# Perceiver block: first cross-attention in two groups of heads, the second group's maxima taken inside the first group's pass

## The reference

```python
q = (x @ Wq + bq).reshape(B, N, 16, 16)      # 128 queries, 16 heads of 16
k = (y @ Wk + bk).reshape(B, M, 16, 16)      # M = 12544 keys
v = (y @ Wv + bv).reshape(B, M, 16, 16)
scores = einsum('bnhd,bmhd->bhnm', q, k) * 0.25
out = einsum('bhnm,bmhd->bnhd', softmax(scores, -1), v).reshape(B, N, 256)
return relu(out @ W1 + b1) @ W2 + b2
```

## Time and profile before

| what | value |
|---|---|
| median of 3 runs | 1448.72 us (1447.15 to 1449.62) |
| span of the profiled execution | 1446.7 us, 2.0 us under that median |
| busy share of the span | PE 93%, ACT 77%, DVE 74%, POOL 14% |
| chain that ended last | PE 77%, DVE 13%, issue 5%, ACT 3% |
| first attention, first pass | to 258.2 us |
| first attention, second pass | 258.2 to 462.5 us |

### The profile page before, as it was taken

The page is one execution under the profiler, slowest core; times in us unless marked ns, Lnnn a source line. Parts: engine busy times, 40 slices in busy tenths (PEclk is TensorE's granted clock), DMA queues, the critical chain, the costliest instruction groups (busy, mean ns, idle before and its releaser), DMA issues.

```text
span 1446.7 us, 37819 instructions
## 1 busy us (share of the span) xinstructions
PE 1352.2 (93%) x15593; PEld 886.5 (61%) x15593; DVE 1072.6 (74%) x1556; ACT 1120.0 (77%) x1646; POOL 197.9 (14%) x195
## 2 busy tenths in 40 slices
PE   5888888999999998999999979999999999999988
PEld 2444444677776694333333357777777777777768
DVE  6899999100000777999999998888888888788864
ACT  4787877899997466888888868888887888788831
POOL 6322311000000006000000000000000004431630
PEclk9999999999999999999999999999999999999999
DMA  4355434876755564556655576777877588898910
GB/s 144 137 190 186 159 137 145 210 178 147 184 140 155 198 226 149 191 190 227 219 186 189 187 149 133 145 140 154 154 153 146 115 172 181 169 187 170 237 54 5
DMA packets 128849, 236.56 MB, mean 164 GB/s; under 512 B 9292, under 2 KB 114214, under 8 KB 128678
## 3 DMA queue, kind: packets, MB, share of 16 engines
q1 hardware_dynamic: 128678, 234.13, 61.1%
HBM read 155.98 MB, written 78.12 MB: 162 GB/s over the span
## 4 chain that ended last, share of the span: by engine, by line
PE 77%; DVE 13%; issue 5%; ACT 3%; DMA 1%; SPq 1%; POOL 0%; POOLq 0%; DVEq 0%; ACTq 0%
PE ps L794 77%; DVE small L1573 4%; DVE W L1507 3%; DMA W<-in_ctx_dram 1%; DVE p L1507 1%; ACT W L1311 1%; DVE W L1537 1%; DVE q_all L1507 1%; ACT p L1326 1%; DVE ctxT_b L1559 0%; DVE q_all L1817 0%; ACT p L1288 0%; ACT ps L1288 0%; DVE ctxT_a_lo L1563 0%; DVE v L1507 0%
## 5 line engine op out<-in xcount | busy, mean ns | idle before, releaser
L1507 DVE TENSOR_TENSOR p<-ps,p 128x512 f16<-128x512 f32 (+1 forms) x467 | 350.9, 752 | 66.2 <-ACT ps L1288 63.1
L1288 ACT ACTIVATE p<-ps 128x512 f16<-128x512 f32 (+1 forms) x490 | 329.4, 682 | 83.4 <-PE ps L794 81.0
L794 PEld LDWEIGHTS ps<-q_all,W 128*128 128x128 f16 (+1 forms) x3544 | 228.8, 99 | 71.5 <-issue 12.7
L794 PE MATMUL ps<-q_all,W 128*128 128x128 f16 (+2 forms) x3544 | 262.5, 226 | 8.8 <-DVE p L1507 5.3
L1288 ACT ACTIVATE ps<-ps 128x512 f32<-128x512 f32 x392 | 236.0, 602 | 0.0
L794 PE MATMUL ps<-v,p 128*128 128x130 f16 x3136 | 169.3, 206 | 6.3 <-DVE p L1507 2.7
L794 PE MATMUL ps<-wv,ctxT_a_hi 128*128 128x512 f16 (+1 forms) x588 | 155.3, 345 | 10.1 <-DVE W L1537 5.9
L794 PEld LDWEIGHTS ps<-v,p 128*128 128x128 f16 x3136 | 147.3, 97 | 12.7 <-ACT ps L1288 4.0
L1674 DVE COPY att<-ps 128x512 f32<-128x512 f32 x1 | 0.7, 692 | 201.6 <-PE ps L794 201.6
L1507 DVE TENSOR_TENSOR v<-ps,v 128x512 f16<-128x512 f32 x196 | 135.5, 692 | 12.9 <-ACT v L1384 0.5
L794 PE MATMUL ps<-wv,ctxT_b 128*128 128x512 f16 (+1 forms) x504 | 136.1, 338 | 0.1
(11 more groups left out here) (276 smaller groups left out, 2005.4 us busy)
## 6 DMA issues: line engine op xcount, KB each, us to landing
W<-keys_hi SPq DMA_DIRECT2D x54, 896.0 KB, 8.0
W<-keys_low SPq DMA_DIRECT2D x27, 896.0 KB, 11.5
keys_hi<-p SPq DMA_DIRECT2D x75, 224.0 KB, 1.9
keys_low<-p SPq DMA_DIRECT2D x75, 224.0 KB, 1.9
keys_hi<-W SPq DMA_DIRECT2D x65, 224.0 KB, 1.9
keys_low<-W SPq DMA_DIRECT2D x65, 224.0 KB, 1.9
W<-values SPq DMA_DIRECT2D x14, 960.0 KB, 9.2
W<-in_L_ffn_W_dram SPq DMA_DIRECT2D x10, 1024.0 KB, 10.0
```

The costliest lines, as they stand in the source:

```text
L794: return pe.matmul(out_, lhsT, rhs, start=start, stop=stop, **kw)
L1288: return act.activation(out_, in_, ACT.Exp, scale=scale)
L1507: return dve.tensor_tensor(out_, a, b, op)
```

## The change

The first attention's heads become two groups, 0-7 and 8-15.

- **First pass:** `ORDER0` has four pairs a round in place of eight; only heads 0-7 get their maxima there. `running` holds four heads. The last `values` turn is now the last turn of the round. The keys and values of all heads are still projected and stored; values are laid out by group.
- **Second pass, group 0:** per tile one set of 8 heads: 4 score matmuls (slots of two banks, 0-1 and 2-3 in turn), one exponential, 8 weighing matmuls. Tiles go in pairs: scores of two tiles, then weighing of the two before. Between these, at two places per pair, PE scores units of `LATE`: the maxima of heads 8-15, 154 units, 11 per chunk. Heads 8-12 are *whole* units (two matmuls into banks 4 and 5, one reduction of 128 x 896), heads 13-15 are two *half* units each (one matmul into bank 7, one reduction of 128 x 448). A unit waits until DVE has reduced the last unit of its own kind (`late_reduced`). The units are spread over the first 94 of 98 places (`LATE_SPREAD`).
- **Between the groups:** the group's shifts are formed, turned by PE into bank 7 and written to `q_one`.
- **Second pass, group 1:** 98 tiles again, three slots for scores.
- **DMA:** SP also reloads the f16 keys of heads 8-15 once (`load_late`); keys get four buffers, values three, each for one group. Three `load_late` and three `load_values0` of half size are queued in the first pass, each just ahead of the next round's context load.

```diff
-        ORDER0 = ("keys1 pair ab values lo pair values pair values pair pair values pair pair keys0 pair").split()
+        ORDER0 = "keys1 pair ab values lo pair values pair values keys0 pair values".split()
...
+        WHOLE, HALVES = 5, 3
...
+        def late_units():
+            units = []
+            for c in range(NCH):
+                whole = [(c, G0 + h, None) for h in range(WHOLE)]
+                halves = [(c, G0 + WHOLE + h, k) for h in range(HALVES) for k in range(2)]
+                for a, b in zip(whole, halves):
+                    units += [a, b]
+                units += halves[WHOLE:]
+            return units
...
+        LATE_SPREAD = 2 * (PAIRS0 - 2)
+        def bank0(g, t):
+            return t % 2 * 2 if g == 0 else t % 3 * 2
...
-                if c in (4, 5):
+                if c in (4, 5, 6):
                     load_values0(c - 4)
+                if c in (7, 8, 9):
...
+                    load_late(c - 7)
...
+            def score_late(j):
+                c, h, half = LATE[j]
+                if before := late_before(j):
+                    pe.wait_ge(late_reduced, before)
...
+                for k in (0, 1) if half is None else (half,):
+                    ins = mm(ps[:, 4 + k if half is None else T0_BANK, 0:MAXC], q_max[:, h * P:(h + 1) * P],
+                             late_keys[c % 3][:, k * MAXC:(k + 1) * MAXC], True, True)
+                ins.then_inc(late_scored, 1)
...
-                for t in range(NT + 1):
-                    if t < NT:
-                        for j in range(2):
...
+                for g in range(2):
+                    for p in range(PAIRS0 + 1):
+                        if p < PAIRS0:
...
+                            score0(g, 2 * p)
+                            score0(g, 2 * p + 1)
+                        for place in range(2):
+                            if g == 0:
+                                upto = min(-(-len(LATE) * (2 * p + place + 1) // LATE_SPREAD), len(LATE))
+                                while done < upto:
+                                    score_late(done)
+                                    done += 1
+                            if p and place == 0:
+                                weigh0(g, 2 * p - 2)
+                                weigh0(g, 2 * p - 1)
...
+            def late_maxima():
+                for j, (c, h, half) in enumerate(LATE):
+                    dve.wait_ge(late_scored, j + 1)
+                    if half is None:
+                        ins = dve.tensor_reduce(late_whole[:, h - G0, c:c + 1], ps[:, 4:6, 0:MAXC], AX.XY, ALU.max)
+                    else:
+                        k = 2 * c + half
+                        ins = dve.tensor_reduce(late_halves[:, h - G0 - WHOLE, k:k + 1], ps[:, T0_BANK, 0:MAXC], AX.X,
+                                                ALU.max)
+                    ins.then_inc(late_reduced, 1)
```

More of the change, by code:

```diff
@@ L369, in turn_left @@
             return [(max_copied, N_COP[L.n, n, h])]
[L372 to L376, removed]
+        KW0_HOMES = stage[:, 0:3584], W[:, 1536:5120]
+        KW0 = [r[:, 1792 * k:1792 * (k + 1)].bitcast(F16).rearrange("p (s k) -> p s k", s=4)
+               for r in KW0_HOMES for k in range(2)]
@@ new lines, in late_units, with late_before @@
+        def late_units():
[7 more added lines that the diff above has]
+            return units
+        LATE = late_units()
+        LATE_PER_CHUNK = len(LATE) // NCH
+        def late_before(j):
+            same = [n for n in range(j) if (LATE[n][2] is None) == (LATE[j][2] is None)]
+            return same[-1] + 1 if same else 0
@@ L597, in load_expert0 @@
                 load_blocks(ld_exp0[e], EXPERT0[e][1], d["L0_ffn_W2"][e])
-            for c in range(2, NCH):
-                load_keys0(c)
-                load_values0(c)
+            for n in range(3, 2 * NCH):
+                if n < NCH:
+                    load_late(n)
+                load_values0(n)
+                if n + 1 < 2 * NCH:
+                    load_keys0(n + 1)
             sp.wait_ge(scored, 2 * NT)
@@ L918, in first_pass, with score0 @@
                     mm(ps[L.shift_rows, O0_BANK, 0:P], shift_pair, ident[:, :], True, True).then_inc(shift_turned, 1)
[L920 to L926, removed]
+            def score0(g, t):
+                i, n = g * NT + t, g * NCH + t // CH
+                bank = bank0(g, t)
+                if g and t == 2:
+                    pe.wait_ge(late_reduced, len(LATE))
+                elif i >= 2:
+                    pe.wait_ge(exped, i - 1 if g == 0 or t < 2 else i - 2)
+                if t % CH == 0:
+                    pe.wait_ge(ld_group[n % 4], 48 * (n // 4 + 1))
@@ L927, in score0 @@
                 own = slice(t % CH * P, (t % CH + 1) * P)
[L928 to L931, removed]
+                for s in range(4):
+                    ins = mm(ps[:, bank + s // 2, s % 2 * 256:(s % 2 + 1) * 256], KW0[n % 4][:, s, own],
+                             q_one[:, (4 * g + s) * 256:(4 * g + s + 1) * 256], True, True)
@@ L1361, in attend0 @@
                 load_exp_table()
-                for t in range(NT):
-                    for j in range(2):
-                        n = 2 * t + j
-                        act.wait_ge(scored, n + 1)
-                        if t >= 2:
-                            act.wait_ge(weighed, t - 1)
-                        exp(p_whole[t % 2][:, j * 1024:(j + 1) * 1024].rearrange("p (b k) -> p b k", b=2),
-                            ps[:, n % 3 * 2:n % 3 * 2 + 2, :], 1.0 / VS).then_inc(exped, 1)
+                for g in range(2):
+                    for t in range(NT):
+                        i, bank = g * NT + t, bank0(g, t)
+                        act.wait_ge(scored, i + 1)
+                        if i >= 4:
+                            act.wait_ge(weighed, i // 2 - 1)
+                        exp(p_whole[i % 4].rearrange("p (b k) -> p b k", b=2), ps[:, bank:bank + 2, :],
+                            1.0 / VS).then_inc(exped, 1)
             def attend1():
@@ L1606, in first_pass, with shift0 @@
-                    for n in range(2):
-                        heads = slice(8 * n, 8 * (n + 1))
-                        tt(q_one[rows, n * 1024:(n + 1) * 1024].rearrange("p (h q) -> p h q", h=8),
-                           bc(ps[rows, O0_BANK, 0:P], 1, [32, 8, P]), bc(by16[rows, heads], 2, [32, 8, P]),
-                           ALU.mult).then_inc(rows_made, 1)
+                    shift0(0)
+                    place_shift0(0, O0_BANK)
+            def shift0(g):
+                own = slice(G0 * g, G0 * (g + 1))
+                mx, hi16 = mx_all[:, own], shift_hi[:, own]
+                settle(ts(mx, mx, -1.0 / VS, EXP_SHIFT, ALU.mult, ALU.add))
+                settle(dve.tensor_copy(hi16, mx))
+                dve.tensor_copy(shift_pair[:, own], hi16)
+                tt(shift_pair[:, H + G0 * g:H + G0 * (g + 1)], mx, hi16, ALU.subtract).then_inc(shift_made, 1)
```

180 lines of the change are left out of this document (110 added, 70 removed).

## The result

| | before | forecast | after |
|---|---|---|---|
| median, us | 1447.93 (4 runs, 1446.36 to 1449.62) | 1493 (1471 to 1513) | 1507.46 (4 runs, 1507.14 to 1511.31) |
| ratio to before | | | 1.042 [1.040, 1.043] |
| span of the profiled execution | 1446.7 | 1491.5 | 1509.6 |
| first pass, to the first scores | 258.2 | 240.0 | 267.6 |
| second pass | 204.3 | 267.3 | 259.4 |

The change makes the kernel 4.2% slower. The two stretches miss in opposite directions: the first pass by +27.6 us, the second by -7.9.

What follows compares the result with a forecast made beforehand. It took DVE to bound the first pass and PE the second, ACT close behind. Second pass +63.0, first pass -16 and -2.2: net +44.8 on span 1446.7 gives 1491.5, median 2.0 above: 1493 us, range 1471 to 1513.

Steps and rivals of the forecast that it cites:

- the load loop: First pass: context load, cast, last values copy, next load set the nine rounds that wait for a load; no gain there.
- the likeliest case: Whole kernel: the main forecast, median 1493 us with 1483 to 1503 of its own; chance 0.57.
- the rival of worse coupling: Both passes: loads take 6.5 us (12 more over nine), PE waits 24 for DVE, not 16; 1513 us, chance 0.18.
- the 9.6: First pass: us from cast to end of last values copy, 8.27 before, with one pair (0.48) replaced by `keys0` (1.80).
- Ring order: First pass DMA: key stores issued right behind a context load do not delay it, so its 5.2 us stands.
- The slots' walk: First pass: walking the turns with their waits for PSUM slots gives 13.8 us a round, without the load's limit.
- loop does not bind: First pass rival: nine rounds at 13.8 us save 20.7 more; kernel 1473 us, chance 0.16.
- The fold: End of first pass: folding four heads takes 2.1 us where eight took 4.24; with it a gain of 2.2.
- coupling 16: Second pass, group 0: PE waits 16 us for DVE's late reductions, each kind having one home; bounds 8 and 26.
- PE's own sum: Second pass, group 0: scoring and weighing 97 us, late matmuls 42.6, unit starts 3, start and flush 2; 145 us.
- with full rotation the 16 would be 0: Second pass, group 0: if late units rotated through banks, PE's 16 us of waiting for DVE would vanish.
- pauses of PE's own issue: Second pass: 7 us of PE issue pauses before, assumed to stay 7 over both groups.

Runs made afterwards that it cites:

- a_tiny: The changed kernel with DVE's late reductions reading only the first 8 columns, homes and waits kept; 1490.71 us, ratio 1.030.
- a_hold: The changed kernel, with SP issuing the key stores only after the context load ahead of them has landed, from round 1 on; 1491.93 us, ratio 1.031.
- a_early: The changed kernel with each context load queued one round earlier, behind the key stores and ahead of the values stores; 1464.65 us, ratio 1.012.
- a_rot: The changed kernel with every late unit a half unit, in banks 4, 5 and 7 in turn; 1491.25 us, ratio 1.030.

## Why the prediction was right in kind and off in size

**The sign and the two causes held.** PE pays for the late maxima in the second pass, and the load loop takes back the first pass. 1507.46 is inside the range and beyond the likeliest case's own 1483 to 1503. It lies near the rival of worse coupling, 1513, but not for its reasons: its loads (12 us more over nine) came to some 4 us, and its 24 us between PE and DVE stayed at 17 to 19. What took their place, the lower clock, stands in no rival, and the second pass erred 7.9 us the other way. That the total fell inside the range is in part luck. The first pass as a whole did not gain 18.2 us but lost 9.4.

**First pass: the nine rounds were mis-sized.** The step that failed is the 9.6 in "Loop: 9.6 + 0.45 + 5.2 = 15.3 us", the way from cast to values copy, which was taken at full clock in all nine rounds. In the one loop with a full clock the sum holds: 15.43 us. Eight of the nine rounds stand between the load issues at 51.68 and 204.22: 19.1 us each, where the forecast has 16.2, 23 us in all. PE's pieces behind the cast are 58.5 us for eight times 5.29, so 16 of the 23 are slower matmuls. The eight loads take 50.3 us where the forecast, with its reloads ahead, has 46.2: 4 more. The last 3 are spread over the rest of the way. The other 4 of the 27.6 us are in the ninth round and in the start and end, and were not taken apart. The 16 belong to this one profile: `a_tiny`, with the same first pass, has 9 by the same count.

**Ring order.** The Trainium skill ("DMA: Bandwidth & Descriptors", Queues, rings and completion order) has descriptors consumed in ring order, and from that the forecast concluded that stores behind a load do not delay it. The runs contradict this conclusion: landing takes 5.7 us in the median with the stores behind, 5.1 with them held back (`a_hold`). What is queued behind takes something from what is ahead. Still the forecast's loads (5.2, 6.35 and 5.75 us, 5.8 on average) are nearer to the 6.2 measured in the loop than the rival's, which are 1.3 us longer each.

**The clock was not in the sum at all.** I had read the clock as full in both stretches and carried it over, though the forecast itself put ACT's wait before the cast at some 3 us a round, which PE must then wait too. In the profile of before the longest wait of PE for that copy (L1343) is 1.1 us, at full clock, so it could not be learnt there; the forecast should have named it as an unknown.

**Without the loop, the rounds were right.** The slots' walk gave 13.8 us, and after has 13.7 in its round without a load, `a_early` 13.6. The rival "loop does not bind" gave 1473; `a_early` measures 1464.65, with 48 us from the first pass's end.

**End of the pass.** The fold took 2.49 us for 2.1, against 4.24.

**Second pass, group 0.** Forecast 161, measured 159.9. Its parts: coupling 16, measured 16.7 as the difference to `a_tiny` and 18.6 to `a_rot`; that leaves 143.2 for PE's own sum, forecast 145. The assumption that 448 columns on all rows cost 0.19 us held well enough to be within 2 us over 224 of them.

**Rotation.** The rule that independent groups rotate through banks (the Trainium skill, "Perfetto Trace Analysis", Optimizing Tensor Performance, Matmuls) was weighed as "with full rotation the 16 would be 0". As far as the runs can tell it is: group 0 takes 142.6 us in `a_rot` and 144.5 in `a_tiny`, whose reductions take 0.17 us each.

**Between the groups and group 1.** 1.3 for 1.8, and 98.2 for 97.5.

**The pauses: 7 us that did not come.** The forecast carried over 7 us of pauses of PE's own issue. The chain through group 1 of after is one piece:

```profile
430.54 93.73 PE ps L856 x1880
```

while the chain of before in its second pass has six gaps, of which two are

```profile
310.44 0.81 issue
...
410.56 1.90 issue
```

and which add up to 5.4 us. So the term was a little too large, and group 1 of after has none of it. Nothing here was run on why; PE's instruction stream is another one (a loop over pairs of tiles and two groups), and key reloads are of half size. It stays open.

**Carried to the kernel's end.** The rest of the kernel is 1.6 us shorter, and the median of after lies 2.1 us under its profiled span, where 2.0 above was assumed; the profiled run was the slowest of four.

## What to carry to other kernels

When a change shortens the round of the engine that bounds it, look for the circle that the round was covering: from a buffer's last read, through an in-order DMA queue, to the next use. Here it was 15 us long by forecast and in its first round, and up to 20 in the others, mostly because PE's matmuls slowed behind the wait. One line in the DMA queue's list, or one turn in the order, took 43 to 46 us off the kernel. Queue a load by the time it is needed, ahead of whatever must wait for this round's output. A unit that hands PSUM from PE to DVE and waits for its return wants more than one home; one home for each of two kinds cost 17 us over 154 units, and three in turn took it back.

## What was not expected of the hardware

- In rounds of some 20 us with a wait of about 4 us on PE the granted clock is 0.83 over the round. In `a_hold`, with waits of 1 to 3 us, it is 0.94 from the first to the last load, and with idle matmuls in the wait 1.00. The idle matmuls made the kernel 12 us faster. The length of the wait alone does not tell: behind 3.89 us in `a_tiny` four matmuls of a pair take 0.55 us, behind 3.90 us in after 0.93. The same first pass lost 9 us more in one profile than in another this way.
- Stores of 224 KB, the first two issued within 1.1 us behind a load of 672 KB, lengthen it: median landing 5.7 us with them and 5.1 without.
- PE's issue pauses of up to 1.90 us in the second pass of before, none in group 1 of after; not explained.
